# Rows of wo scaled to powers of two, and its third matmul product made conditional

## The reference, cut to what matters

```
x = x + attn(_layernorm(x))
x = x + ffn(_layernorm(x))

def attn(x):
    x = x + linear_attention(layernorm(x, g1, b1), wq, wk, wv, wo)
    h = layernorm(x, g2, b2)
    return x + lookup_gelu(h @ w1) @ w2

def linear_attention(x, wq, wk, wv, wo):
    ...
    out = (num / den).reshape(B, S, D)
    return out @ wo

def ffn(x):
    return (x @ CB.T) * (SCB / 127) + bias
```

## Time and profile before

| | |
|---|---|
| median of 3 runs | 652.83 us (643.82 to 653.84) |
| the profiled execution | 651.4 us |
| its span, first to last instruction | 649.6 us |
| PE busy | 90% of the span |
| DVE busy | 80% |
| ACT busy | 63% |
| POOL busy | 59% |
| mean granted TensorE clock | 0.975 of full speed |

### The profile page before, as it was taken

The page is one execution under the profiler, slowest core; times in us unless marked ns, Lnnn a source line. Parts: engine busy times, 40 slices in busy tenths (PEclk is TensorE's granted clock), DMA queues, the critical chain, the costliest instruction groups (busy, mean ns, idle before and its releaser), DMA issues.

```text
span 649.6 us, 12205 instructions
## 1 busy us (share of the span) xinstructions
PE 586.2 (90%) x3838; PEld 517.6 (80%) x3838; DVE 517.0 (80%) x1076; ACT 411.7 (63%) x767; POOL 386.2 (59%) x337
## 2 busy tenths in 40 slices
PE   6999999999997999898998989989899898998875
PEld 6887787878786878788787978879788797887675
DVE  5488988898873688878888788887988878888656
ACT  2377767676765685675756757576665766657560
POOL 3446475655542447676486765757657576675553
PEclk8599999999997999999999999999999999999898
DMA  8101112021101000000100001010110000100001
GB/s 287 53 34 65 59 38 65 32 65 34 66 1 36 17 32 33 32 32 32 65 32 32 33 33 65 32 32 32 32 65 32 32 32 32 65 24 11 33 1 67
DMA packets 11128, 29.16 MB, mean 45 GB/s; under 512 B 2016, under 2 KB 4576, under 8 KB 11104
## 3 DMA queue, kind: packets, MB, share of 16 engines
q1 hardware_dynamic: 9472, 28.32, 12.3%
q10 hardware_dynamic: 1632, 0.53, 0.4%
HBM read 20.45 MB, written 8.39 MB: 44 GB/s over the span
## 4 chain that ended last, share of the span: by engine, by line
PE 36%; DVE 27%; issue 16%; POOL 12%; ACT 6%; DMA 1%; DVEq 1%; ACTq 0%; POOLq 0%; SPq 0%
PE psum L914 31%; DVE f_arena L729 8%; POOL f_arena L355 5%; DVE bn_stats L615 5%; PE psum L932 4%; POOL rstd L324 3%; DVE f_arena L755 3%; DVE f_arena L657 2%; DVE mean_var L622 2%; ACT grid_index L540 2%; DVE f32r_arena L738 2%; POOL pow_arg L322 2%; ACT f32r_arena L550 2%; ACT f32r_arena L494 1%; DVE f_arena L642 1%
## 5 line engine op out<-in xcount | busy, mean ns | idle before, releaser
L914 PE MATMUL psum<-w_hi,f32r_arena 128*128 128x256 f32 x1280 | 178.7, 286 | 5.1 <-DVE f32r_arena L738 3.5
L914 PEld LDWEIGHTS psum<-w_hi,f32r_arena 128*128 128x128 f32 x1280 | 164.9, 190 | 16.0 <-issue 11.5
L914 PE MATMUL psum<-f32r_arena,w_hi 128*128 128x512 f32 x512 | 143.0, 411 | 3.7 <-issue 3.7
L540 ACT ACTIVATE grid_index<-psum,w_bias_in_steps 128x512 int8<-128x512 f32 x128 | 87.2, 681 | 69.9 <-PE psum L914 69.9
L729 DVE TENSOR_SCALAR f_arena<-f_arena,mean_var,rstd 128x256 f32<-128x256 f32 x124 | 102.7, 887 | 25.9 <-POOL rstd L324 25.9
L914 PE MATMUL psum<-f32r_arena 128*128 128x512 f32 (+1 forms) x512 | 120.5, 378 | 2.6 <-issue 1.5
L343 POOL TENSOR_TENSOR f32r_arena<-f_arena,f32r_arena 128x512 fp32r<-128x512 f32 x64 | 86.0, 1344 | 56.3 <-ACT f32r_arena L550 56.3
L914 PEld LDWEIGHTS psum<-f32r_arena,w_hi 128*128 128x128 f32 x512 | 91.1, 194 | 22.4 <-ACT grid_index L540 4.7
L932 PE MATMUL psum<-ident,f_arena 128*128 128x128 f32 x504 | 69.6, 283 | 36.9 <-DVE f_arena L729 32.3
L932 PEld LDWEIGHTS psum<-ident,f_arena 128*128 128x128 f32 x504 | 58.6, 145 | 52.1 <-issue 28.3
L914 PEld LDWEIGHTS psum<-f32r_arena 128*128 128x128 f32 x512 | 83.2, 190 | 14.9 <-issue 3.1
(11 more groups left out here) (96 smaller groups left out, 976.4 us busy)
## 6 DMA issues: line engine op xcount, KB each, us to landing
f_arena<-in_L_attn_x_dram SPq DMA_DIRECT2D x32, 512.0 KB, 3.3
out_dram<-f_arena SPq DMA_DIRECT2D x15, 512.0 KB, 2.6
f_arena<-in_L_attn_w_dram SPq DMA_DIRECT2D x2, 1024.0 KB, 11.3
out_dram<-f_arena SPq DMA_DIRECT2D x2, 256.0 KB, 2.2
phi_q<-in_L_attn_wk_dram ACTq DMA_DIRECT2D x1, 256.0 KB, 4.9
phi_q<-in_L_attn_wv_dram ACTq DMA_DIRECT2D x1, 256.0 KB, 5.4
phi_q<-in_L_attn_wq_dram SPq DMA_DIRECT2D x1, 256.0 KB, 5.7
phi_q<-in_L_ffn_CB_dram SPq DMA_DIRECT2D x1, 256.0 KB, 7.8
```

Of the source, the lines that this page charges most:

```text
L540: act(k8[:, m % 2], bank(AB + m % 2), ACT.Identity, scale=1.0 / STEP, bias=h_bias[:, m:m + 1]).then_inc(s["grid_ready"], 1)
L914: return nc.tensor.matmul(out_, lhs, rhs, start=start, stop=stop, skip_group_check=True)
```

## The change

Each row of wo is divided by its largest absolute value (`wo_scale`, its reciprocal `wo_inv`), which gives `wo_hi` and, from the rest, `wo_lo`. Rows of wo are the features of the attention rows, which lie on partitions after the transposes, so the same scale multiplies the attention rows when their halves are made: ACT's `high` takes it as a scale per partition, DVE's `low` becomes a multiply and subtract in one instruction. The largest magnitude of `wo_lo` joins the second flag as a seventh column, and in phase 2 `attention_out` leaves the third product out where the flag is zero. In phase 1 (chunk 0) it stays. ACT's copy of wo is gone; POOL makes all parts after its third `power1`.

```diff
+            def split_wo():
+                g.wait_ge(s["wo_inverse"], 1)
+                for k in range(KT):
+                    nc.gpsimd.tensor_scalar(fm(wo_hi[:, :])[:, k], fm(wo_raw)[:, k], wo_inv[:, k:k + 1], 0.0, ALU.mult,
+                                            ALU.add).then_inc(s["wo_hi_done"], 1)
+                g.wait_ge(s["wo_hi_done"], KT)
+                for k in range(KT):
+                    nc.gpsimd.tensor_scalar(fm(wo_rest[:, :])[:, k], fm(wo_hi[:, :])[:, k].bitcast(F32), wo_scale[:, k:k + 1], 0.0,
+                                            ALU.mult, ALU.add).then_inc(s["wo_parted"], 1)
+                g.wait_ge(s["wo_parted"], KT)
+                nc.gpsimd.tensor_tensor(wo_rest[:, :], wo_raw, wo_rest[:, :], ALU.subtract).then_inc(s["wo_left"], 1)
+                g.wait_ge(s["wo_left"], 1)
+                for k in range(KT):
+                    nc.gpsimd.tensor_scalar(fm(wo_lo[:, :])[:, k], fm(wo_rest[:, :])[:, k], wo_inv[:, k:k + 1], 0.0, ALU.mult,
+                                            ALU.add).then_inc(s["wo_lo_done"], 1)
...
             power1(2, 0)
+            split_wo()
...
-            a.wait_ge(loaded["wo"], 16)
-            act(wo_hi[:, :], wo_raw, ACT.Copy).then_inc(s["wo_hi_done"], 1)
...
                 for k in range(KT):
-                    act(fm(dst)[:, k], bank(b + k), ACT.Copy).then_inc(s[done], 1)
+                    act(fm(dst)[:, k], bank(b + k), ACT.Copy,
+                        scale=wo_scale[:, k:k + 1] if done == "s_hi_a" else 1.0).then_inc(s[done], 1)
...
             stats1(2, 0, 1)
+            v.wait_ge(loaded["wo"], 16)
+            for k in range(KT):
+                i = ve.tensor_reduce(wo_scale[:, k:k + 1], fm(wo_raw)[:, k], AX.X, ALU.max, apply_absolute_value=True)
+            i.then_inc(s["wo_max"], 1)
+            v.wait_ge(s["wo_max"], 1)
+            ve.tensor_scalar(wo_scale[:, :], wo_scale[:, :], 1e-30, None, ALU.max).then_inc(s["wo_scaled"], 1)
+            v.wait_ge(s["wo_scaled"], 1)
+            ve.reciprocal(wo_inv[:, :], wo_scale[:, :]).then_inc(s["wo_inverse"], 1)
...
-                    ve.tensor_tensor(fm(lo_)[:, k], bank(b + k), fm(hi_)[:, k].bitcast(F32), ALU.subtract).then_inc(s[done], 1)
+                    if done == "s_lo_a":
+                        ve.scalar_tensor_tensor(out=fm(lo_)[:, k], in0=bank(b + k), scalar=wo_scale[:, k:k + 1],
+                                                in1=fm(hi_)[:, k].bitcast(F32), op0=ALU.mult,
+                                                op1=ALU.subtract).then_inc(s[done], 1)
...
-            v.wait_ge(s["w_flag"], SLICES)
-            flag_column(2, SLICES, 3 + SLICES)
+            v.wait_ge(s["wo_lo_done"], KT)
+            ve.tensor_reduce(flag_cols[:, 2 + SLICES:3 + SLICES], wo_lo[:, :].bitcast(F32), AX.X, ALU.max,
+                             apply_absolute_value=True).then_inc(s["w_flag"], 1)
+            v.wait_ge(s["w_flag"], SLICES + 1)
+            flag_column(2, SLICES + 1, 4 + SLICES)
...
-                            attention_out(0)
+                            attention_out(0, True)
...
-                        attention_out(i + 1)
+                        attention_out(i + 1, not exact)
...
-    nc = _bacc.Bacc("TRN2", target_bir_lowering=False, num_devices=1)
+    nc = _bacc.Bacc("TRN2", target_bir_lowering=False, num_devices=1, dynamic_dma_scratch_size=1024)
```

More of the change, by code:

```diff
@@ L95, in build @@
         wo_lo = sb("wo_lo", [P, KT * D], F32R)
+        wo_rest = sb("wo_rest", [P, KT * D])
+        wo_scale, wo_inv = sb("wo_row_scale", [P, KT]), sb("wo_row_scale_inverse", [P, KT])
         stats_all = sb("ln0_scale_shift", [P, CHUNKS * 2 * TT])
@@ L103, in build @@
         minus_half = sb("minus_half", [P, 2 * TT])
-        flag_cols = sb("flag_cols", [P, 2 + SLICES + 2])
+        flag_cols = sb("flag_cols", [P, 2 + SLICES + 3])
         flags = sb("flags", [1, 2])
@@ L180, in build @@
             wkv_lo_done tables_ready w2_half xb_half xp_half bn_half mv_half u_half pow_half n_half turned_half s_hi_half s_lo_half cb_half ot_half out_half
-            wo_lo_done flag_col flag_max flag_turned flag1 flag2 w_hi_done w_lo_done w_flag ones_made
+            wo_max wo_scaled wo_inverse wo_parted wo_left wo_lo_done flag_col flag_max flag_turned flag1 flag2 w_hi_done w_lo_done w_flag ones_made
             bn1 mv1_ready u1_ready pow1 shift1 shift1_kept n1_ready n1_turned a1_ready hi1 lo1 kv_tile q_ready
@@ L314, in _ @@
                                         pattern=[[-sign * HEAD, GH]], channel_multiplier=sign).then_inc(s["masks_made"], 1)
-            g.wait_ge(s["wo_hi_done"], 1)
-            nc.gpsimd.tensor_tensor(wo_lo[:, :], wo_raw, wo_hi[:, :].bitcast(F32), ALU.subtract).then_inc(s["wo_lo_done"], 1)
+            def split_wo():
[13 more added lines that the diff above has]
+                                            ALU.add).then_inc(s["wo_lo_done"], 1)
             def power(c, u, r, mv, ready, arg, done):
@@ L685, in _ @@
             v.wait_ge(s["flag_col"], 1)
-            flag_column(0, 2, 2 + SLICES)
+            flag_column(0, 2, 3 + SLICES)
             high1(0, 0)
@@ L744, in low @@
                     v.wait_ge(s[ready], c * KT + (k + 1))
-                    ve.tensor_tensor(fm(lo_)[:, k], bank(b + k), fm(hi_)[:, k].bitcast(F32), ALU.subtract).then_inc(s[done], 1)
+                    if done == "s_lo_a":
+                        ve.scalar_tensor_tensor(out=fm(lo_)[:, k], in0=bank(b + k), scalar=wo_scale[:, k:k + 1],
+                                                in1=fm(hi_)[:, k].bitcast(F32), op0=ALU.mult,
+                                                op1=ALU.subtract).then_inc(s[done], 1)
+                    else:
+                        ve.tensor_tensor(fm(lo_)[:, k], bank(b + k), fm(hi_)[:, k].bitcast(F32), ALU.subtract).then_inc(s[done], 1)
             def attn_low(c):
@@ L1028, in pair @@
                             pe.wait_ge(s["a1_ready"], c + 2)
-                            pe.wait_ge(s["wo_lo_done"], 1)
-                            attention_out(0)
+                            pe.wait_ge(s["wo_lo_done"], KT)
+                            attention_out(0, True)
                         if is_chunk(c, CHUNKS - 1):
@@ L1041, in pair @@
                             pe.wait_ge(s["flag_max"], 2)
-                            turn_flag(3 + SLICES, KV)
+                            turn_flag(4 + SLICES, KV)
                         if is_chunk(c, CHUNKS - 1):
@@ L1087, in rows, with attention_out @@
                 return i
-            def attention_out(c):
+            def attention_out(c, narrow):
                 pe.wait_ge(s["s_hi_a"], c * KT + KT)
                 pe.wait_ge(s["s_lo_a"], c * KT + KT)
-                rows(of_chunk(c, SB2, AB), of_chunk(c, s_hi, s0_hi), of_chunk(c, s_lo, s0_lo), woh, wol, True).then_inc(s["o_done"], 1)
+                rows(of_chunk(c, SB2, AB), of_chunk(c, s_hi, s0_hi), of_chunk(c, s_lo, s0_lo), woh, wol, narrow).then_inc(s["o_done"], 1)
             def turn2(c):
@@ L1219, in _ @@
             pe.wait_ge(s["flag_max"], 1)
-            turn_flag(2 + SLICES, QB)
+            turn_flag(3 + SLICES, QB)
             def project_bias():
```

## The result

The changed kernel takes 658.21 us (median of 5 runs, 655.01 to 659.78) against 651.89 us for the kernel before (median of 5 runs beside it): ratio 1.0135, 95% interval [1.009, 1.018]. The ratio is formed from the fast runs alone; the quotient of the two medians is 1.0097. The changed kernel is slower, by less than 2%. The forecast was 658. The profiled execution is the quickest of the five, 655.01 us with a span of 653.3 us.

What follows compares the result with a forecast made beforehand. The prediction took a ring of waits through all four engines, not PE, to bound phase 2's loop. Its terms: 651.4 + 3.3 (halves) + 0.1 (chunk 0) + 0.8 (flag) + 0.1 (split) + 2.4 (clock) = 658.1 us; range 647 to 668.

Steps and rivals of the forecast that it cites:

- What bounds the loop: Phase 2's loop: waits through all four engines bound it, though PE is busy for 90% of the span.
- The ring of waits: Phase 2: PE's products, ACT's high half, DVE's low half and mean_var, POOL's power and xz, DVE's normalise, residual, norm2, PE again.
- The third product at 0: Phase 2, bodies 0 to 14: eight matmuls fewer gain 0 us; PE's wait grows from 1.54 to 2.49 us.
- PE is the bound after all: Rival for phase 2: all 14.3 us saved would arrive, giving 641.4 us, 1.5% faster; chance 0.08.
- The dearer halves: ACT's and DVE's scaled halves of the attention rows: 0.22 us a body, 3.3 us in phase 2.
- The flag column: End of phase 1's loop: DVE's added reduction of 512 columns delays PE, +0.7 us, +0.8 with the hand-over.
- The split at the start: Making wo's parts on DVE and POOL: by the median it fits POOL's idle 6.12 us; +0.1 us, ends -0.6 and +2.7.
- The sum without falls: Whole kernel without the clock term: 651.4 us plus 4.3 us of added costs, 655.7 us.
- The clock: 4 falls of 0.6 us: Behind PE's 2.49 us wait in bodies 1 to 14: the granted clock falls in four bodies, 2.4 us in all.
- The clock falls in every turn: Rival at PE's wait for the last norm's transposes, bodies 1 to 14: 664.1 us, or 679.5; chance 0.14.
- The change doesn't do what it says: Rival: scaled wo's low half is not exactly zero, so w1, w2, CB regain third products; some 750 us, chance 0.04.

Runs made afterwards that it cites:

- The saving alone: The kernel before with only the third wo product left out in bodies 0 to 14 of phase 2: 649.79 us, ratio 0.9998.
- one exchange on the ring: The kernel before with DVE's mean_var put ahead of the low half of the attention rows in phase 2: 633.18 us, ratio 0.9732.
- the last two runs: Kernel before, then changed kernel, each with DVE's mean_var ahead of the attention low half and POOL's xz ahead of its first mlp_low: 642.36 and 615.63 us.
- the plain halves: The changed kernel with neither half of the attention rows scaled, so the output lacks the scale of wo: 650.82 us, ratio 1.0012.
- The three variants with scaled halves: The changed kernel with eight dummy matmuls before PE's wait for the last norm (1.0031), with the third product put back (1.0047), with four dummies (1.007).
- run again: The changed kernel measured a second time, nothing altered, beside the kernel before: 659.51 us, ratio 1.0159.
- two moves on the ring: DVE's mean_var ahead of the attention low half, POOL's xz ahead of its first mlp_low, in both kernels: before 642.36 us, changed 615.63 us.
- the best order found without it: The kernel before with only DVE's mean_var put ahead of the attention rows' low half: 633.18 us, ratio 0.9732.
- the two variants with turns of 27.28 and 27.29 us: The kernel before without the third product in bodies 0 to 14 (649.79 us), and the changed kernel with unscaled halves (650.82 us).
- the kernel before with both moves: The kernel before with DVE's mean_var ahead of the attention low half and POOL's xz ahead of its first mlp_low: 642.36 us, ratio 0.9873.

## Why the prediction was right, step by step

*What bounds the loop.* Right. The ring of waits was read from the chain, against PE's 90%. The saving alone gained nothing, and one exchange on the ring gained 2.7%.

*The third product at 0.* Right: 0.9998, and the wait 2.44 to 2.48 us where 2.49 was forecast. The rival "PE is the bound after all" falls for this order of the work. Once the ring is shorter PE's work does count, as the last two runs show: in the last one PE is busy for 24.1 of the 25.03 us of a turn.

*The dearer halves, 0.22 us a turn, 3.3 us.* Right in place, a little high: 27.48 against 27.32 is 0.16, against the plain halves 0.19. Single instructions came as priced (ACT 684 ns, DVE 743 ns by the median of each form).

*The flag column, +0.8.* Right: 0.73 us more wait of PE (0.70 to 1.43).

*The split at the start, +0.1.* POOL's seven instructions ran from 25.31 to 31.25 us, and `low1(1)` began right behind them at 31.22, earlier than before the change. But the hole did not hold them. In this execution the input of `low1(1)`, DVE's cast L666, was there earlier as well:

```profile
28.47 0.78 DVE L666 CAST f32r_arena<-f_arena 128x1024 fp32r<-128x1024 f32 x1 [1.95 <-ACT f_arena L462]
...
31.22 2.39 POOL L299 TENSOR_TENSOR f32r_arena<-f_arena,f32r_arena 128x1024 fp32r<-128x1024 f32 x1
```

It was ready at 29.25 us, so the seven held `low1(1)` back by nearly 2 us. PE shows no wait for L299 in the first 60 us, so none of it reached PE. How large this term is in the time cannot be told, since the starts of executions differ by more; the two profiles of before and after differ there by 2 us, the other way.

*The sum without falls* was 651.4 + 4.3, a ratio of 1.0066. The three variants with scaled halves in whose profiles no long turn shows had 1.0031, 1.0047 and 1.007.

*The clock: 4 falls of 0.6 us.* Here the term failed in its size. "Some 0.6 us of a fall reach the ring" stopped at `turn2`, where 0.45 us arrived. It did not follow the late CB product to DVE, and from there to the order of DVE and POOL, where 2 us more are lost. A fall costs 2.4 us. Against that, two of the 14 waits were followed by one in each profile, and not four. So 2 x 2.43 = 4.9 us stand where 2.4 stood, and a long turn is 2.6 us above the turn before the change where 0.8 was forecast. That the total held is in part luck. With the measured terms the sum is 651.4 + 2.4 + 0.1 + 0.7 + 4.9 = 659.5 us. The profiled execution took 655.01, mostly since its start and end were 3.3 us shorter, and the median of 658.21 meets the forecast to 0.1 us while the executions spread from 655.01 to 659.78.

*The clock falls in every turn.* Wrong: two of the 14 waits were followed by a fall, in either profile. The loop that the Trainium skill describes (TensorE: Matmul & The Clock Gate, HAM oscillation) falls back at every turn, behind waits longer than any in the loops here (2.53 us at most), so no run tests it. The rival's limit was a little off too: 2% is passed from (664.4 - 655.7) / 14 = 0.62 us a turn, not 0.7. The numbers of falls in runs without a profile were not seen; that there are some two or more is argued from the 5.3 us between the medians. The mean granted clocks fit more rather than fewer: 0.969 to 0.973 in the other four executions of the changed kernel against 0.978 in the profiled one, and 0.966 to 0.972 against 0.975 when it was run again. In both batches the profiled execution is the quickest. Where the others lost the clock, in the loop or at the start, is not shown.

*The change doesn't do what it says.* Wrong: the flag was zero. The wo products of phase 2 run with `wo_hi` alone, and the time of some 750 us did not come.

## What to carry to other kernels

Before a product is removed, look at the first wait of its engine behind it: if another engine ends that wait, the work becomes wait, however busy the engine is on the page. Then find the ring and shorten that first; the saving that gained nothing here was worth 26.7 us after two moves on the ring, and 17.6 us against the best order found without it. And where DVE and POOL start long SBUF instructions within some tenths of a microsecond of each other, see who comes first in each turn: that order can cost more than the work which is argued about.

## What the runs showed of the hardware

A delay of 0.8 us at DVE's L831 (8.34 instead of 7.56 us behind the transposes) turned into 2.4 us for PE, because a subtraction with two SBUF inputs came behind POOL's sum of 1024 columns. In the loops of all twelve profiles (230 to 600 us, without body 15), DVE's subtraction took 0.68 to 1.06 us where it started 0.10 to 0.66 us ahead of the sum, and the sum 2.65 to 2.86 us. Where it started 0.06 to 0.13 us behind, it took 2.77 to 2.88 us, and the sum 2.34 to 2.40. So DVE pays 2.1 to 2.2 us in the one order, and POOL 0.3 to 0.5 in the other.

The clock's falls do not follow from the length of the wait alone. Behind 14 waits of up to 2.44 us the clock fell twice in each of the two profiles of the changed kernel. Behind waits of 2.37 to 2.53 us it did not fall in the loops of the two variants with turns of 27.28 and 27.29 us. Waits of up to 0.59 and up to 1.50 us, at turns of 27.47 to 27.50, had no fall behind them. Yet in the kernel before with both moves it fell twice in the loop, behind waits of 1.82 and 1.80 us. The first of them, and the stretch behind it (granted clock third from the right):

```profile
253.56 1.19 PE L913 MATMUL psum<-w_hi,f32r_arena 128*128 128x256 f32 x8 [1.82 <-DVE f32r_arena L737]
...
256.00:260.00 4.00, 4.00 (x18) 3.26 (x17) 2.17 (x10) 3.33 (x6) 3.65 (x3) 0.72 0.08 12
```

What else decides it stays open: apart from the changed kernel itself the runs show one profile of each variant, and none was made to test the turn's length by itself.
